# Second norm, masked heads, running sums and weight splits moved in a four-part fused block of layers

## The reference, cut to what matters

```python
xn = _layernorm(x)
x = x + scan_block(xn) + expert_block(xn)        # block 0
xn = _layernorm(x)
x = x + log_linear_attention(xn) + recurrent_ffn(xn)   # block 1

# scan block, per token: a decay and a recurrence over the sequence
xi, z = split(xn @ W_in);  delta = softplus((xi @ W_xp)[..., :1])
h_t = exp(delta_t * A) * h_{t-1} + B_t * xi_t
y = (C * h + D * xi) * silu(z);  y @ W_out
# attention, 16 heads: scores * decay(cumsum of gates) * level weight, then a norm with ln_g, ln_b
o = Y @ Wout.T + x;  (o - mean) * rsqrt(var + 1e-5) * ln_g + ln_b
# recurrent part: the cell runs over the 16 sequences, one step each
c = f * c + i * g;  h = tanh(x @ wo.T + c_final @ uo.T + bo)
```

## Time and profile before

| what | value |
|---|---|
| median of 3 runs | 1022.07 us (1021.91 to 1022.53) |
| the profiled execution | 1022.31 us |
| its span, first to last instruction | 1020.5 us |
| PE busy | 969.2 us (95%) |
| PEld busy | 708.1 us (69%) |
| DVE busy | 858.9 us (84%) |
| ACT busy | 704.3 us (69%) |
| POOL busy | 254.9 us (25%) |
| mean granted clock of PE | 0.990 |

### The profile page before, as it was taken

How to read it: one execution, slowest core, us unless ns; L and a number is a source line. 1 busy time by engine, 2 the same in 40 slices (tenths; PEclk the granted TensorE clock), 3 DMA queues, 4 the chain that set the end, 5 groups by cost and what they waited for, 6 DMA issues and landing times. The chain is left out here.

```text
span 1020.5 us, 20931 instructions
## 1 busy us (share of the span) xinstructions
PE 969.2 (95%) x6894; PEld 708.1 (69%) x6894; DVE 858.9 (84%) x2156; ACT 704.3 (69%) x1528; POOL 254.9 (25%) x319
## 2 busy tenths in 40 slices
PE   6879999999999999999999999999999999999995
PEld 3656767767676777768677676766767677776763
DVE  6888797988979798897979979798897979889777
ACT  4575784939579494866939577593957849396684
POOL 0042021220222122021312212132122212202367
PEclk9989999999999999999999999999999999999997
DMA  4000000000000000000000000000000000000526
GB/s 159 18 4 1 22 2 23 8 21 10 0 31 0 21 10 10 21 0 31 0 21 10 0 31 0 31 0 21 10 0 31 0 21 10 10 21 0 196 77 202
DMA packets 31909, 27.62 MB, mean 27 GB/s; under 512 B 1553, under 2 KB 25745, under 8 KB 31761
## 3 DMA queue, kind: packets, MB, share of 16 engines
q1 hardware_dynamic: 31888, 27.37, 8.3%
HBM read 15.57 MB, written 11.80 MB: 27 GB/s over the span
## 5 line engine op out<-in xcount | busy, mean ns | idle before, releaser
L1115 ACT ACTIVATE gx<-p 128x512 f32<-128x512 f32 x256 | 146.5, 597 | 2.1 <-PE p L628 0.5
L626 PE MATMUL p<-x1Th,Gl 128*128 128x512 f32 x256 | 107.7, 421 | 0.0
L628 PE MATMUL p<-x1Th,Gh 128*128 128x512 f32 x256 | 101.4, 396 | 0.0
L627 PE MATMUL p<-x1Tl,Gh 128*128 128x512 f32 x256 | 100.6, 393 | 0.0
L1979 POOL TENSOR_TENSOR vp<-vdw,e 128x256 f32<-128x256 f32 (+3 forms) x80 | 55.1, 724 | 162.3 <-DVE ms L1663 162.3
L1063 ACT ACTIVATE gelu<-p,bias_u 128x512 f32<-128x512 f32 x32 | 22.0, 688 | 105.3 <-PE p L550 105.3
L748 PEld LDWEIGHTS p<-vbd,pair 128*128 128x128 f32 x512 | 62.0, 191 | 40.4 <-issue 26.8
L748 PE MATMUL p<-vbd,pair 128*128 128x128 f32 x512 | 73.3, 286 | 0.0
L2040 POOL TENSOR_TENSOR skip<-skip,W 128x512 f32<-128x512 f32 x15 | 19.2, 1279 | 215.4 <-DVE skip L1467 215.4
L688 PEld LDWEIGHTS p<-rs,GT 128*128 128x128 f32 x512 | 60.7, 191 | 16.8 <-ACT ms L1198 14.6
L1069 ACT ACTIVATE sm<-mv 128x4 f32<-128x4 f32 x31 | 6.3, 204 | 91.4 <-DVE mv L1462 91.0
(11 more groups left out here) (340 smaller groups left out, 2855.6 us busy)
## 6 DMA issues: line engine op xcount, KB each, us to landing
xin<-in_x SPq DMA_DIRECT2D x16, 256.0 KB, 2.8
hx_scratch<-vdw SPq DMA_DIRECT2D x15, 256.0 KB, 2.6
res_scratch<-normed SPq DMA_DIRECT2D x14, 256.0 KB, 2.0
gx<-in_weights SPq DMA_DIRECT2D x1, 1216.0 KB, 9.4
vp<-hx_scratch SPq DMA_DIRECT2D x4, 256.0 KB, 3.8
GT<-res_scratch SPq DMA_DIRECT2D x4, 256.0 KB, 3.4
out<-vp SPq DMA_DIRECT2D x4, 256.0 KB, 3.5
W<-in_weights SPq DMA_DIRECT2D x1, 746.0 KB, 10.5
```

What stands on the lines that cost most here:

```text
L626: pe.matmul(head_bank(h)[:, :], tile(Gl, h), x1Th[:, :], start=True, stop=False)
L627: pe.matmul(head_bank(h)[:, :], tile(Gh, h), x1Tl[:, :], start=False, stop=False)
L628: pe.matmul(head_bank(h)[:, :], tile(Gh, h), x1Th[:, :], start=False, stop=True).then_inc(R["gx_ps"], 1)
L1115: act.activation(tile(gx, h, T), head_bank(h)[:, :], ACT.Copy).then_inc(R["gx_copied"], 1)
```

## The change

- `norm2(i - 1)` on DVE moves ahead of `own_heads(i, 2)` and `level_sum(i, 2)`.
- `own_heads(i, 0)` moves ahead of `level_weights(i)`.
- `running_sums` is cut in two: the second matmul (`carried_sums`) comes after head 7, and `left_ends` comes ahead of `deltas`.
- `deltas` for sequences 1 to 15 becomes three fp32r matmuls with `Mdh`, `Mdl` (one column each, repeated by its address pattern) and waits for `xsplit_ready`.
- The splits of the weights leave `first`: those of the scan (`Mdelta`, `Win`, `MBC`) run on POOL in `stages(0, 1)` after `xh_ready` of sequence 1, the others after `split_rows`.
- On DVE `node_vectors` moves ahead of `gates_low_part`; its second half, `node_coefficients`, goes into `stages(0, 1)` between `lam_sum` and `fold_own`.
- In `last()` ACT copies head 0 first and `lam_logs` after head 3; the last norm works in the PSUM bank `P1[3]` instead of SBUF; SP stores sequences 13 and 14 ahead of the two halves of 15.

```diff
             def deltas(j):
-                pe.matmul(P0[0][:, :], Mdelta[:, :], xnT[:, :], start=True, stop=True).then_inc(R["delta_ps"], 1)
+                column = lambda t: spread(t[:, 0:1], [128, 128])
+                if not later(j):
+                    pe.matmul(P0[0][:, :], column(Mdelta), xnT[:, :], start=True, stop=True).then_inc(R["delta_ps"], 1)
+                    return
+                pe.wait_ge(R["wsplit_steps"], 6)
+                pe.wait_ge(R["xsplit_ready"], 2 * j)
+                pe.matmul(P0[0][:, :], column(Mdl), xnTh[:, :], start=True, stop=False)
+                pe.matmul(P0[0][:, :], column(Mdh), xnTl[:, :], start=False, stop=False)
+                pe.matmul(P0[0][:, :], column(Mdh), xnTh[:, :], start=False, stop=True).then_inc(R["delta_ps"], 1)
...
                 pe.matmul(P1[2][:, 0:64], upto[:, :], g, start=True, stop=False)
+
+            def carried_sums(i):
+
                 pe.wait_ge(R["gsum_steps"], 2 * i + 2)
...
                     running_sums(i)
                     heads(i, 7, 8)
+                    carried_sums(i)
                 if j is not None:
                     logits(j)
+                if i is not None:
+                    left_ends(i)
+                if j is not None:
                     deltas(j)
                 if i is not None:
-                    left_ends(i)
                     heads(i, 8, 12)
...
                 values(i)
                 gate_logs(i)
+                heads(i, 0, 1)
+                rstd2(i - 1)
+                heads(i, 1, 4)
                 lam_logs(i)
-                rstd2(i - 1)
-                heads(i, 0, 4)
...
                 later_weights()
+                node_vectors()
                 gates_low_part()
...
                 heads_low_part(1)
-                node_vectors()
...
                     lam_sum(i)
+                    if not later(i):
+                        node_coefficients()
                     fold_own(i)
...
                 if i is not None:
+                    own_heads(i, 0)
                     level_weights(i)
-                if i is not None:
-                    own_heads(i, 0)
                     pair_weights(i, 1)
...
                 if i is not None:
+                    if later(i):
+                        norm2(i - 1)
                     own_heads(i, 2)
                     level_sum(i, 2)
-                    if later(i):
-                        norm2(i - 1)
                     pair_weights(i, 3)
...
+            last_ob = P1[3]
...
+                dve.wait_ge(R["ym_ready"], 4 * B)
+                dve.tensor_tensor(last_ob[:, cols], (P0[2], P1[2])[half][:, 0:256], xn1[:, cols], ALU.add)\
+                    .then_inc(R["ob_ready"], 1)
...
-                    last = dve.scalar_tensor_tensor(tile(skip, n), tile(ob, n), mv2[:, 2 * n:2 * n + 1], w("lng"),
+                    last = dve.scalar_tensor_tensor(tile(last_ob, n), tile(last_ob, n), mv2[:, 2 * n:2 * n + 1], w("lng"),
...
+            def split_scan_weights():
+
+                pool.wait_ge(R["z1_ps"], 1)
+                pool.wait_ge(R["xh_ready"], 2)
+                split_weights(((Mdh, Mdl, Mdelta[:, :]), (Winh, Winl, w("Win")), (MBCh, MBCl, MBC[:, :])), 0)
+
+            def split_other_weights():
+
+                pool.wait_ge(R["u1_ps"], 1)
                 pool.wait_ge(R["vdw_ps"], TILES)
                 pool.wait_ge(R["gates_xl_ready"], 1)
...
+                split_weights(((W1h, W1l, w("W1")), (Wvh, Wvl, w("Wvdw", 0, 336)), (gates_ch, gates_cl, w("gates_c"))), 6)
...
             def stages(i, j):
+                if not later(i):
+                    split_scan_weights()
                 split_inputs(j)
                 level_values(i)
                 split_rows(i, j)
+                if not later(i):
+                    split_other_weights()
                 split_cell(i, 2 * i + 2)
...
-                split_weights()
```

More of the change, by code:

```diff
@@ L125, in build @@
         MB, MC = MBC[:, 0:INNER], MBC[:, INNER:2 * INNER]
-        Mdelta = sb("Mdelta", 128)
+        Mdelta = sb("Mdelta", 1)
+        Mdh = sb("Mdh", 1, fp32r)
+        Mdl = sb("Mdl", 1, fp32r)
         Gh = sb("Gh", H * 128, fp32r)
@@ L358, in last @@
                     store(b, whole, end_hx[b])
+                for b in (13, 14):
+                    sp.wait_ge(R["end_pool_add"], END_POOL.index(b) + 1)
+                    store(b, whole, end_hx[b])
                 for half in range(2):
@@ L361, in last @@
                     store(B - 1, slice(2 * half, 2 * half + 2), end_hx[B - 1])
-                    sp.wait_ge(R["end_pool_add"], END_POOL.index(13 + half) + 1)
-                    store(13 + half, whole, end_hx[13 + half])
                 sp.wait_ge(R["end_stored"], 16 * (B + 1))
@@ L512, in scan_x @@
                 if later(j):
-                    pe.wait_ge(R["wsplit_steps"], 10)
+                    pe.wait_ge(R["wsplit_steps"], 6)
                     pe.wait_ge(R["xsplit_ready"], 2 * j)
@@ L542, in gate_u @@
                 else:
+                    pe.wait_ge(R["wsplit_steps"], 12)
                     pe.wait_ge(R["hsplit_ready"], 2 * j)
@@ L969, in first @@
                 act.wait_ge(R["setup_ps"], 1)
-                act.activation(Mdelta[:, :], P1[1][:, 0:128], ACT.Copy).then_inc(R["setup_ev"], 1)
+                act.activation(Mdelta[:, :], P1[1][:, 0:1], ACT.Copy).then_inc(R["setup_ev"], 1)
                 turned_h(0)
@@ L1405, in node_vectors, with node_coefficients @@
                 step(last)
+            def node_coefficients():
                 step(dve.memset(ones_to[:, 0:1], 1.0))
@@ L1878, in last_attention_out @@
                 dve.wait_ge(R["res_ready"], B - 1)
-                dve.tensor_tensor(ob[:, cols], (P0[2], P1[2])[half][:, 0:256], xn1[:, cols], ALU.add).then_inc(R["ob_ready"], 1)
+                dve.wait_ge(R["ym_ready"], 4 * B)
+                dve.tensor_tensor(last_ob[:, cols], (P0[2], P1[2])[half][:, 0:256], xn1[:, cols], ALU.add)\
+                    .then_inc(R["ob_ready"], 1)
             def last_stats(half):
@@ L1884, in last_stats @@
                 for n in (2 * half, 2 * half + 1):
-                    last = dve.bn_stats(st2[:, 6 * n:6 * n + 6], tile(ob, n))
+                    last = dve.bn_stats(st2[:, 6 * n:6 * n + 6], tile(last_ob, n))
                 last.then_inc(R["st2_ready"], 1)
@@ L1905, in last_out @@
                 for n in (2 * half, 2 * half + 1):
-                    done = dve.scalar_tensor_tensor(tile(end_hx[B - 1], n), tile(skip, n), sm2[:, 4 + n:5 + n],
+                    done = dve.scalar_tensor_tensor(tile(end_hx[B - 1], n), tile(last_ob, n), sm2[:, 4 + n:5 + n],
                                                     tile(end_hx[B - 1], n), ALU.mult, ALU.add)
@@ L2017, in split_cell, with split_weights @@
                 pool.tensor_tensor(celll[:, :], cell[:, :], cellh[:, :], ALU.subtract).then_inc(R["csplit_ready"], 1)
-            def split_weights():
+            def split_weights(parts, done):
+                for n, (high, low_part, whole) in enumerate(parts):
+                    pool.tensor_copy(high[:, :], whole).then_inc(R["wsplit_steps"], 1)
+                    pool.wait_ge(R["wsplit_steps"], done + 2 * n + 1)
+                    pool.tensor_tensor(low_part[:, :], whole, high[:, :], ALU.subtract).then_inc(R["wsplit_steps"], 1)
+            def split_scan_weights():
[4 more added lines that the diff above has]
+                pool.wait_ge(R["u1_ps"], 1)
                 pool.wait_ge(R["vdw_ps"], TILES)
                 pool.wait_ge(R["gates_xl_ready"], 1)
[L2023 to L2028, removed]
+                split_weights(((W1h, W1l, w("W1")), (Wvh, Wvl, w("Wvdw", 0, 336)), (gates_ch, gates_cl, w("gates_c"))), 6)
             def keep_skip(i):
```

4 lines of the change are left out of this document (2 added, 2 removed).

## The result

| | before | after |
|---|---|---|
| median | 1022.48 us (5 runs, 1021.91 to 1023.48) | 1027.43 us (5 runs, 1026.58 to 1028.60) |
| profiled execution, its span | 1020.5 us | 1025.6 us |
| one iteration of the loop | 60.47 us | 60.90 us |

The change makes the kernel slower by half a per cent: the ratio is 1.0048, with an interval of 1.0034 to 1.0063. The two spans differ by 5.1 us, the medians by 4.95. The iteration is read from POOL's first split of a stage, which stands at 486.98 and, seven stages later, at 913.28; 426.30 / 7 = 60.90.

A forecast was written before the change was run, and what follows sets the result against it. DVE, then POOL, was taken to set the end of each stage's second half, with PE only following. Loop +4.6, first stage -0.7 and end -2.1 gave +1.8 us, a median of 1023.9 us, range 1018 to 1030.

The forecast's parts named there:

- Second half, `norm2`: Loop, second half of a stage: `norm2` delays `levels(3)` and `out0`, POOL's residual comes earlier; +0.41 us an iteration.
- The swap: Loop, second half: `own_heads(0)` ahead of `level_weights` saves PE about 0.4 us, all of it slack.
- First half: Loop, sums, ends and deltas: PE's wait moves to head 11, `vp` limits the gain; -0.08 us, bounds -0.3 and +0.2.
- First stage: Runs once: PE's 5.50 us wait for xn goes, most of the gain is swallowed; -0.7 us, bounds -4 and +1.
- End: Last norm and stores: norm in PSUM is faster, the last store follows the data; -2.1 us, bounds -1.2 and -2.6.
- The new order of ACT's copies: Start of `last()`: frees PE 0.5 us, but the `vp` row bounds that stage; 0, bounds -0.3 and +0.2.
- slower by more: Whole kernel: slower by more than the 2.0 us (0.2%) that a measurement tells from no change; chance 0.42.
- Rival (d): Second half: `norm2` costs its full 0.83 us an iteration, in all 1029.8 us; chance 0.2 together with (e).
- Rival (a): Second half: POOL's earlier residual counts in full, `sum0` 0.42 us earlier, in all 1012 us; chance 0.15.
- Rival (b): Whole loop: PE is the bound throughout, its savings reach the end, -18 us, in all 1001; chance 0.05.
- (c): First stage: it keeps most of its 5.5 us, -4 instead of -0.7, in all 1020.6 us; chance 0.15.
- (e): First half: each new wait is late, +0.2 us, in all about 1028 us; chance 0.2 together with Rival (d).

The follow-up runs named there:

- experiment 1: The changed kernel with `norm2` back in its old place behind `level_sum(2)`, the rest kept: 1019.76 us, ratio 0.9979.
- experiment 2: The kernel before with only `norm2` moved ahead of `own_heads(2)`: 1030.10 us, ratio 1.0070.
- experiment 7: The kernel before with only `own_heads(0)` moved ahead of `level_weights`: 1022.95 us, ratio 1.0002.
- experiment 10: The kernel before with only `carried_sums` behind head 7 and `left_ends` ahead of the deltas, which stay fp32: 1023.64 us, ratio 1.0020.
- experiment 11: The kernel before with only the weight splits and node vectors moved and the deltas from fp32r parts: 1019.84 us, ratio 0.9977.
- experiment 5: On experiment 4: head 8 ahead of deltas (PE) and delta passes (ACT), ACT's last two head copies ahead of `pair_distance`: 1020.08 us, ratio 0.9975.
- experiment 6: On experiment 5: `attention_out` moved behind the node copies, ACT's two second-norm steps ahead of the left halves: 1025.53 us, ratio 1.0024.
- experiment 8: The kernel before with only the last norm in PSUM and the new order of the last stores: 1021.57 us, ratio 0.9992.
- experiment 4: On experiment 3: POOL's finishing row waits until DVE has made the second gated half `y1`: 1014.48 us, ratio 0.9922.
- experiment 3: The changed kernel with `norm2` early, before the third `pair_lams`, its statistics behind the node copies: 1052.21 us, ratio 1.0289.
- experiment 9: On experiment 4: ACT's two second-norm steps one place earlier, ahead of the first left halves: 1013.63 us, ratio 0.9915.

## Why the prediction came out as it did

**Second half, `norm2`: right, the mechanism link by link.** Forecast: `levels(3)` +0.83, POOL's residual 1.76 earlier, `sum0` +0.41, `turn_x1` takes up the rest. Measured: +0.89, -1.78, +0.47, +0.47. DVE's wait at `sum0` is 2.15 us long and names PE, as announced, and PE waits 1.03 us at L771. Experiments 1 and 2 show that this move alone carries the loss. The 0.06 lies at `levels(3)`: it starts 0.14 us after the products of `level_sum(2)` end (282.35 against 281.60 + 0.61), where the sum had put 0.05; 14 times 0.06 is 0.8 us.

**The swap: right.** It is slack (experiment 7).

**First half: right in mechanism, -0.03 instead of -0.08.** The wait moved to head 11 as forecast, for ACT's copy of head 8. The 0.08 is there at `pair_scores(0)` and is lost by the end of the left halves, whose fourth tile waits for `vp` (PE's weight load of L676 0.2 us for POOL), as announced. Two sizes were off. The copy of the sums moved by 0.07 us and not by 0.21, since it stands behind a DVE operation that ends at about the same time. And the three matmuls of the deltas take 0.79 us from start to start (246.15 to 246.94), not 0.69:

```profile
246.15 0.48 PE L502 MATMUL p<-xnTh,Mdl 128*128 128x512 f32 x1
...
246.94 0.40 PE L638 MATMUL p<-x1Th,Gl 128*128 128x512 f32 x1
```

The order of sums and ends brings nothing by itself (experiment 10); the deltas from parts bring 0.11 us in the old order (experiment 11), under half of the 0.24 that was estimated for a kernel bound by PE from the rule of the Trainium skill (FP8 and Floating Point Precision, TensorE Precision Notes), and the new order hides most of that too (60.42 us in experiment 1). What I had not seen is how tight ACT is; experiments 5 and 6, built on the thought that DVE's row alone would be next, lost 0.4 us each.

**First stage: -0.27 instead of -0.7, inside its bounds, for another reason than given.** The wait of 5.50 us is gone and the gain was swallowed. xn is ready 5.7 us earlier (50.96 instead of 56.63), and the three gate steps at 1.29, 0.52 and 1.31 us and the node steps in the row to `vp` (1.85 us) are as forecast. The copy of the sums is at 59.28 and not near 58.5: DVE waits 1.96 us there for PE, whose clock stands at half. That the clock falls stood only at the end of the bounds. By the stretches of experiment 11 the stage is 0.45 us shorter with the early fall of the clock in both kernels and 2.0 us shorter without it, and the start of a single profile varies by more than all this. So it is in part luck that -0.27 lies near -0.7.

**End: wrong, -0.8 instead of -2.1, outside its bounds of -1.2 to -2.6.** L1896 was right to 0.03 us, but the four pairs of DVE operations take 2.51 us from 1018.52 and not 2.2. The step that failed is that the last store follows the last data, 0.5 us behind it: the four stores end the kernel, and the DMA engines under them were idle for only 0.8 us before the change (experiment 8). The new order of ACT's copies is worth nothing, as forecast: from POOL's last first split to `last_attention_out` it is 100.68 us before and 101.10 after, the 0.4 of one iteration.

**Sum.** Forecast +4.6 - 0.7 - 2.1 = +1.8; measured +6.2 - 0.3 - 0.8 = +5.1. All three terms erred to the same side: 1.6 us from 0.11 us in each of 14 iterations, 0.4 and 1.3. The result lies in the range, in its upper quarter, at the edge of the forecast's own range of 1021 to 1027.5, and in the case "slower by more", which had 0.42. Rival (d), the full 0.83 an iteration, falls: the slack at `turn_x1` gave back 0.42. Rival (a) falls as well, but only for this place: with `norm2` out of the way and POOL held back, `sum0` does follow `out0` (experiment 4). Rival (b) falls, and (c) too: the first stage gives 0.3 us, and some 2.0 where the clock holds, not 4. Of (e) nothing is seen, the first half is not longer.

The Trainium skill says (SBUF - State Buffer, Who interferes with whom) that a DVE instruction with two SBUF inputs contends with a POOL one that reads SBUF. The trace agrees: 0.22 us becomes 1.29, the length of the POOL operation beside it (1.28). It also says that a DVE instruction with at most one SBUF input, outside the 2-port perf modes, does not contend, and that copy, cast and `tensor_scalar` can enter these modes. The prediction leaves that limit out, and it counts here: a reciprocal with one input keeps its 0.55 us, but the four `tensor_scalar` of the earlier trace rows take 3.04 us beside POOL instead of 1.11, and the cast L1547 of experiment 3 0.87 instead of 0.23.

## What to carry to other kernels

Before moving a step on an engine whose row has no gap, find the operation behind it that another engine waits for, and count the moved length there in full; the step that was to come earlier (here POOL's residual, by 1.78 us) is worth only what it was last by. A producer that runs free on an idle engine can be worse than one that waits: when it runs decides which of its neighbour's small operations it stops. And if one step is to go, look for the place where its engine waits for another (here 1.2 us before the pair products), not for the place nearest to its consumer.

## What was new about the hardware

- A wait of PE of 1.7 to 2.4 us was followed by a stretch at half clock (1.2 GHz) in some executions and iterations and not in others: in five of thirteen iterations of experiment 3 (1.0 us each), and in the first stage of the changed kernel but not of experiments 1 and 11. What it cost there ran from 0.2 us (experiment 9) to 0.9; an earlier fall of the clock, behind waits of 0.87, 0.81 and 0.69 us that runs without the fall have too, cost 1.4. A term that rests on such a wait has more than one value. The Trainium skill (TensorE: Matmul & The Clock Gate, Part 1) describes a clock that is halved after low activity of the array; this case shows that the same program can meet it or not.
- The issue of the last four stores took 0.37 to 0.49 us each where the DMA engines had just had a gap, and 0.84 to 0.87 us each where they were busy throughout at 282 to 291 GB/s, also for stores of half the size (1.74 us for two of 128 KB). Earlier data wins no more at the end than these engines were idle.
- POOL's finishing row of 4.1 us cost DVE nothing beside operations that read PSUM, and 2.3 us an iteration beside `top1` (62.34 against 60.01 us).
